# State product of a gated linear attention on four 64x64 places, value product in two parts

## The chip, the core and the metric

The kernel runs on one NeuronCore of a Trainium2 chip. The metric is the device time of one execution in microseconds (us). All engines of the core are in use: TensorE (PE in the profile) multiplies, VectorE (DVE), ScalarE (ACT) and GpSimd (POOL) do the rest, SyncE (SP) issues most transfers. TensorE writes its products to eight PSUM banks of 128 partitions x 512 floats.

## What is computed

The input is 4 sequences of 2048 tokens with 256 features. A layer norm is followed by a linear attention with 16 heads of 64 and a decaying state, a gate, an output projection and a residual; then comes a small network that is applied three times, with layer norms around both. The part that the change touches is the attention:

```python
Q = (xn @ WQ.T + bQ); K = (xn @ WK.T + bK); V = (xn @ WV.T + bV)     # 16 heads of 64
gate = silu(xn @ Wg.T + bg)
h = alpha * h + k[:, :, :, None] * v[:, :, None, :]    # token after token, h is 64x64 per head
o = einsum('bhi,bhij->bhj', q, h)
y = (o * gate) @ WO.T + bO
```

## The kernel before

Tokens are taken in **steps** of 512 (`NS` = 4 steps per sequence, 16 in all). A step projects its values first (`values`, 8 products of six matmuls), then goes through `NP` = 8 **pairs** of heads. A pair fills the 128 partitions: head e of the pair has the rows e*64 to e*64+63. Inside a pair the 512 tokens are `NC` = 4 **chunks** of 128, and the recurrence is replaced by matrix products for each chunk:

- `project` makes keys, queries and gate of the pair (six matmuls of 512 columns each, in split precision: high and low halves).
- `scores` multiplies keys and queries in 32-key blocks, each at 64x32 of the array; `masked` on DVE copies the causal part to `att`. In odd chunks the order of the 32-token blocks is reversed (the host prepares it so), so that the two chunks of a couple share one mask.
- `keys_transposed` turns the end-weighted keys `k_end` (made by POOL), ACT copies them to `k_tok` (`tokens_of`), `updates` multiplies them with the values, and DVE carries the state from chunk to chunk (`h_seq`, L758 and L762).
- `from_state` (L929) multiplies the state with the queries. The states of both heads stand in a block-diagonal 128x128 matrix `h_bd`, whose other two quarters are zero: four fp32 products of 128 columns.
- `from_chunk` (L938) adds the values times `att`: for each chunk and head one product of 128 keys, 64 outputs and 128 queries, two heads side by side in the array.
- `gated` on DVE multiplies bank 5 with the gate to `o_g` (L740), ACT and POOL split it into `o_hi` and `o_lo`, and `y_part` (L951, twelve matmuls of 256 columns) adds the pair's share of the output projection to banks 6 and 7.

An fp32 product is issued as two passes, so the trace has two MATMUL and two weight-load rows for each.

The order is written by hand, engine by engine, with semaphores; nothing is scheduled by a tool. TensorE's sequence of a pair p is: keys, queries and gate of pair p+1, `y_part(p-1)`, `from_state(p)`, `keys_transposed` of p+1, `from_chunk(p)`, `updates(p+1)`, `scores(p+1)`. Pair 6 has no `y_part`; pair 7 has two and a third follows the queries and gate of the next step's first pair. `x_transposed` (eight 128x128 transposes of the next step's normed input, in pair 6) and `x1_transposed` (eight of the last step's result, in pair 0) stand between. Banks: 0 and 1 keys, queries and gate in turn, 2 and 3 scores, 4 transposed keys and updates, 5 the output, 6 and 7 the output projection. After four steps comes the small network of that sequence, and `final_transposed` turns its result back.

Of the kernel before, what the change touches and what calls it, by code (L numbers as in the profile page):

```python
# [7 lines left out]
i32 = mybir.dt.int32  # L8
# [24 lines left out]
def build(nc, a, out):  # L33
    ctx = ExitStack()
    with ctx:
# [64 lines left out]
        h_bd = sb("h_bd", [P, NC, P])  # L100
# [41 lines left out]
        def k_bank(p):  # L142

            return p % 2

        def q_bank(p):

            return 1 - p % 2

        def g_bank(n):  # L150

            return n % NP % 2 if n else 5
# [44 lines left out]
        s_hbd = sem("state_diagonal_ready")  # L197
# [45 lines left out]
        started = [s_x1, s_out, s_og, s_xlo, s_upd, s_hbd, s_o, s_x1t, s_qev, s_kev, s_hs, s_x1c, s_ktok, s_att,  # L243
# [80 lines left out]
        def final_rows(t, c):  # L324

            return bank[(2, 0, 4, 6)[t] + c // 2][:, (c % 2) * D:(c % 2 + 1) * D]

        def v_bank(m):

            return bank[(2, 3, 5, 1, 2, 3, 0, 5)[m]]  # L330
# [7 lines left out]
        def _(pool):  # L338
# [47 lines left out]
            for b in range(B):  # L386
                for s in range(NS):
                    it = b * NS + s
                    following = it + 1 < B * NS
                    pool.wait_ge(s_x, (it + 1) * 16)  # L390
                    pool.wait_ge(s_x1, it + C0)
                    nc.gpsimd.tensor_tensor(x_2b[:], x_in[:], bias_o[:].unsqueeze(1).broadcast_to([P, NC, D]),
                                            ALU.add).then_inc(s_x2b, 1)
                    pool.wait_ge(s_x2b, it * 2 + 1)
                    nc.gpsimd.tensor_tensor(x_2b[:], x_2b[:], x_in[:], ALU.add).then_inc(s_x2b, 1)
                    pool.wait_ge(s_x2b, it * 2 + 2)
                    pool.sem_inc(s_xfree, 1)
                    for p in range(NP):
                        n = it * NP + p
                        if p + 1 < NP:  # L400
                            ends_of(p + 1, n + 1)
                        elif following:
                            ends_of(0, n + 1)
                        o_low(p, n)
                        if p == NP - 5 and following:
                            pool.wait_ge(s_stats, it + 2)
                            nc.gpsimd.tensor_tensor(rstd[:], vare[:], half_neg[:], ALU.pow).then_inc(s_rstd, 1)
                    pool.wait_ge(s_r1, it + 1)
# [12 lines left out]
        def _(act):  # L421
# [9 lines left out]
            def x_parts(step, banks_of):  # L431

                for k in range(KT):
                    act.wait_ge(s_xt, step * KT + k + 1)
                    if k == 0:
                        act.wait_ge(s_xlo, step + C0)
                    nc.scalar.activation(x_f[:, k, :], bank[banks_of[k]][:], ACT.Identity,
                                         bias=beta[:, k:k + 1], scale=gamma[:, k:k + 1]).then_inc(s_xf, 1)
                act.wait_ge(s_xf, (step + 1) * KT)
                nc.scalar.activation(x_hi[:], x_f, ACT.Copy).then_inc(s_xhi, 1)  # L440
# [18 lines left out]
            def tokens_of(n, bk):  # L459

                act.wait_ge(s_kt, n + 1 + C0)
                act.wait_ge(s_upd, n + C0)
                nc.scalar.activation(k_tok[:], part(bk, NC), ACT.Copy).then_inc(s_ktok, 1)  # L463

            def states_of(p, n):
# [3 lines left out]
                for e in range(2):  # L469
                    rows = slice(e * DH, (e + 1) * DH)  # L470
                    nc.scalar.activation(h_bd[rows, :, e * DH:(e + 1) * DH], h_seq[rows, :, :],  # L471
                                         ACT.Copy, scale=pows[rows, p, HP:HP + 1]).then_inc(s_hbd, 1)
# [7 lines left out]
            def x1_copied(step, first_bank):  # L480

                place = step % NS
                for k in range(KT):
                    act.wait_ge(s_x1t, step * KT + k + 1 + C0)
                    nc.scalar.activation(x1t[:, k, place * ST:(place + 1) * ST], bank[first_bank + k],
                                         ACT.Copy).then_inc(s_x1c, 1)
# [19 lines left out]
            x_parts(0, (0, 1))  # L506
# [8 lines left out]
            for b in range(B):  # L515
                for s in range(NS):
                    it = b * NS + s
                    following = it + 1 < B * NS
                    tokens_of(it * NP, 4)
                    for p in range(NP):  # L520
                        n = it * NP + p
                        states_of(p, n)
                        if p + 1 < NP:
# [3 lines left out]
                            tokens_of(n + 1, 4)  # L527
                            if p == 0 and s:
                                x1_copied(it - 1, 6)
                            if p == NP - 2 and following:  # L530
                                x_parts(it + 1, (0, 1))
                            o_high(p, n)
                        else:
                            o_high(p, n)
                            if following:
                                queries_shifted(0, n + 1)
                                act.wait_ge(s_og, n + C0)
                                gate_of(0, n + 1)

# [37 lines left out]
                for t in range(NS):  # L577
                    act.wait_ge(s_sh, b * NS + t + 1)
                    for c in range(NC):
                        last = nc.scalar.activation(fin[t][:, c, :], final_rows(t, c), ACT.Identity,  # L580
# [5 lines left out]
        def _(dve):  # L586
            nc.vector.memset(att[:].bitcast(i32), 0).then_inc(s_setv, 1)
            nc.vector.memset(h_bd[:].bitcast(i32), 0).then_inc(s_setv, 1)
            nc.vector.memset(bank[2], 0.0).then_inc(s_setv, 1)
            nc.vector.memset(bank[3], 0.0).then_inc(s_setv, 1)  # L590
# [3 lines left out]
            dve.wait_ge(s_setv, 7)  # L594
# [10 lines left out]
            def norm_stats(src, count, done, mv=mv[:], vare=vare[:]):  # L605

                for c in range(NC):
                    nc.vector.bn_stats(stats[:, c, :], src(c)).then_inc(s_st, 1)  # L608
                dve.wait_ge(s_st, count + NC)
# [589 lines left out]
```

## Time and profile before

| | us |
|---|---|
| median of 3 runs | 1869.63 (1869.55 to 1871.22) |
| the profiled execution | 1871.02 |
| its span, first to last instruction | 1869.3 |
| PE busy | 1792.7 (96% of the span) |
| DVE, ACT, POOL busy | 1076.9, 784.8, 483.1 |

A row of the timeline gives the start and the length of a run of like instructions. Matmuls overlap in the pipeline, so a run's length says little of what it costs; what counts is from the start of one run to the start of the next on the same engine. That is how TensorE's times are read below. The granted clock is at 2.4 GHz in all but the first and the last slice.

### The profile page before, as it was taken

To read this page: it belongs to the slowest core of one execution; us is meant where nothing else is said; L and a number is where in the kernel's file an instruction comes from. 1 tells how busy PE (TensorE), PEld (TensorE's weight loads), DVE (VectorE), ACT (ScalarE), POOL (GpSimd) and SP (SyncE) were. 2 spreads that over 40 slices of the span, in tenths; PEclk is the share of its full clock that TensorE was granted. 3 is DMA by queue.
4 is the path that set the end of the run, shared out by engine and by line. 5 is a ranking of instruction groups with operands and counts; after the bars stand their busy time and mean duration, and the time that the engine had idled before them with its cause. 6 is when DMAs were issued, how large, how long until landed. Compare 5 with 4: busy or idle time off the path is not lost.

```text
span 1869.3 us, 45361 instructions
## 1 busy us (share of the span) xinstructions
PE 1792.7 (96%) x19632; PEld 1383.2 (74%) x19632; DVE 1076.9 (58%) x2214; ACT 784.8 (42%) x1411; POOL 483.1 (26%) x373
## 2 busy tenths in 40 slices
PE   5999999999799999999979999999989999999996
PEld 4888888863588888885368888888438888888742
DVE  7565655555756555555665655555475555555546
ACT  3434343444443434344444343434444434343444
POOL 4232222212223222220222322222022222222202
PEclk9999999999999999999999999999999999999998
DMA  4000000000100000000010000000001000000001
GB/s 151 13 13 2 13 2 13 2 1 0 57 2 13 2 13 2 13 2 1 0 57 2 13 2 13 2 12 2 1 3 55 2 13 2 13 2 2 2 0 46
DMA packets 22823, 26.20 MB, mean 14 GB/s; under 512 B 3168, under 2 KB 21472, under 8 KB 22624
## 3 DMA queue, kind: packets, MB, share of 16 engines
q1 hardware_dynamic: 20624, 19.09, 3.2%
q10 hardware_dynamic: 2000, 4.20, 0.6%
q8 instruction: 156, 2.56, 0.6%
q14 instruction: 43, 0.35, 0.1%
HBM read 14.90 MB, written 8.39 MB: 12 GB/s over the span
## 4 chain that ended last, share of the span: by engine, by line
PE 92%; DVE 4%; ACT 2%; issue 1%; POOL 1%; DMA 0%; DVEq 0%; ACTq 0%; SPq 0%
PE bank L875 39%; PE bank L951 10%; PE bank L1110 9%; PE bank L938 7%; PE bank L902 6%; PE bank L929 6%; PE bank L1127 4%; PE bank L919 3%; PE bank L911 3%; PE bank L1153 1%; PE bank L1140 1%; DVE stats L608 1%; PE bank L866 1%; DVE v_sb L843 1%; PE bank L962 1%
## 5 line engine op out<-in xcount | busy, mean ns | idle before, releaser
L740 DVE TENSOR_TENSOR o_g<-bank,gate 128x512 f32<-128x512 f32 x128 | 88.6, 692 | 441.1 <-PE bank L938 441.1
L379 POOL TENSOR_TENSOR o_lo<-o_g,o_hi 128x512 fp32r<-128x512 f32 x128 | 166.0, 1297 | 659.7 <-ACT o_hi L478 659.7
L453 ACT ACTIVATE q_sb<-q_sb,pows 128x384 f32<-128x384 f32 (+2 forms) x384 | 168.2, 501 | 256.0 <-DVE q_sb L650 256.0
L370 POOL TENSOR_TENSOR k_end<-k_sc,pows 128x512 f32<-128x512 f32 x128 | 135.1, 1056 | 295.4 <-DVE k_sc L641 295.4
L471 ACT ACTIVATE h_bd<-h_seq,pows 64x256 f32<-64x256 f32 x256 | 130.6, 510 | 148.7 <-DVE h_seq L762 145.5
L463 ACT ACTIVATE k_tok<-bank 128x512 f32<-128x512 f32 x128 | 76.6, 598 | 243.6 <-PE bank L911 242.8
L729 DVE COPY_PREDICATED att<-causal,bank 128x1024 f32<-128x1024 int32 x128 | 168.6, 1317 | 6.2 <-PE bank L902 5.4
L478 ACT ACTIVATE o_hi<-o_g 128x512 fp32r<-128x512 f32 x128 | 80.7, 630 | 199.7 <-DVE o_g L740 199.5
L951 PE MATMUL bank<-wo_hi,o_hi 128*128 128x256 f32 x512 | 149.6, 292 | 2.8 <-POOL o_lo L379 2.8
L951 PE MATMUL bank<-wo_hi,o_lo 128*128 128x256 f32 x512 | 145.1, 283 | 0.0
L951 PE MATMUL bank<-wo_lo,o_hi 128*128 128x256 f32 x512 | 144.8, 283 | 0.0
L938 PE MATMUL bank<-att,v_sb 128*64 128x128 f32 x2048 | 140.1, 279 | 0.0
L929 PE MATMUL bank<-q_sb,h_bd 128*128 128x128 f32 x1024 | 137.4, 277 | 0.1
L929 PEld LDWEIGHTS bank<-q_sb,h_bd 128*128 128x128 f32 x1024 | 128.3, 192 | 5.9 <-ACT h_bd L471 3.0
L902 PE MATMUL bank<-q_sb,k_sc 64*32 64x64 f32 (+3 forms) x8192 | 128.1, 236 | 0.0
L938 PEld LDWEIGHTS bank<-att,v_sb 128*64 128x64 f32 x2048 | 109.2, 136 | 24.2 <-issue 24.1
L650 DVE SCALAR_TENSOR_TENSOR q_sb<-bank,col_bias,pows 128x512 f32<-128x512 f32 x128 | 96.1, 751 | 53.7 <-PE bank L875 53.6
L762 DVE SCALAR_TENSOR_TENSOR h_seq<-h_seq,pows,bank 128x64 f32<-128x64 f32 x384 | 107.9, 281 | 24.4 <-PE bank L919 2.0
L1110 PE MATMUL bank<-v_sb,f_w 128*128 128x512 f32 x256 | 121.0, 605 | 0.0
L875 PE MATMUL bank<-x_hi,wk_hi 128*128 128x512 f32 x256 | 113.2, 442 | 0.0
L902 PEld LDWEIGHTS bank<-q_sb,k_sc 64*32 64x32 f32 x8192 | 102.1, 106 | 14.2 <-issue 5.8
L722 DVE TENSOR_TENSOR v_sb<-bank,bias_v 128x512 f32<-128x512 f32 x128 | 85.0, 688 | 46.4 <-PE bank L875 45.7
(145 smaller groups left out, 3830.2 us busy)
## 6 DMA issues: line engine op xcount, KB each, us to landing
x_in<-in_x SPq DMA_DIRECT2D x16, 512.0 KB, 3.9
out_y<-q_sb SPq DMA_DIRECT2D x8, 512.0 KB, 2.8
out_y<-x_nf SPq DMA_DIRECT2D x8, 512.0 KB, 2.9
v_sb<-in_wq ACTq DMA_DIRECT2D x1, 1024.0 KB, 5.0
v_sb<-in_wk SPq DMA_DIRECT2D x1, 1024.0 KB, 8.8
x1t<-in_wg ACTq DMA_DIRECT2D x1, 1024.0 KB, 10.2
x1t<-in_wv ACTq DMA_DIRECT2D x1, 1024.0 KB, 13.1
q_sb<-in_wo ACTq DMA_DIRECT2D x1, 1024.0 KB, 17.1
```

Source lines behind the costliest of these rows:

```text
L370: nc.gpsimd.tensor_tensor(k_end[:].rearrange("p (a z) (b r) -> p a (z b) r", z=2, r=BL), k_sc[:].rearrange("p (a z) (b r) -> p a (z b) r", ...
L379: nc.gpsimd.tensor_tensor(o_lo[:, p % 2], o_g[:, p % 2], o_hi[:, p % 2].bitcast(f32), ALU.subtract).then_inc(s_olo, 1)
L453: last = nc.scalar.activation(q_sb[:, p % 2, d].rearrange("p (a z) n -> p a (z n)", z=2)[:, :, reach], q_sb[:, p % 2, 0].rearrange("p (a z ...
L471: nc.scalar.activation(h_bd[rows, :, e * DH:(e + 1) * DH], h_seq[rows, :, :], ACT.Copy, scale=pows[rows, p, HP:HP + 1]).then_inc(s_hbd, 1)
L729: nc.vector.copy_predicated(att[:].rearrange("p e (a z) n -> p (e a) (z n)", z=2), causal[:].bitcast(i32).rearrange("p z n -> p (z n)").un ...
L762: step = nc.vector.scalar_tensor_tensor(h_seq[:, c + 1, :] if c + 1 < NC else h_st[:, p, :], h_seq[:, c, :], pows[:, p, HP + 1:HP + 2], ba ...
L875: last = nc.tensor.matmul(dst, l(k), r(k), start=(m == 0), stop=(m == 5))
L902: last = nc.tensor.matmul(bank[2 + e][g * BL:(g + 1) * BL, cols:cols + count * BL], k_sc[rows, c, g * BL:(g + 1) * BL], query_blocks(rows, ...
L929: nc.tensor.matmul(bank[5][:, c * C:(c + 1) * C], h_bd[:, c, :], query_blocks(slice(0, P), p, c, first, NB), start=(c == 0), stop=False, s ...
L938: last = nc.tensor.matmul(bank[5][e * DH:(e + 1) * DH, c * C:(c + 1) * C], v_sb[:, c, h * DH:(h + 1) * DH], att[:, e, c, :], start=False, ...
L951: last = nc.tensor.matmul(dst, l[:, p % 2, tok], w[:, p, :], start=(p == 0 and c % 2 == 0 and i == 0), stop=(p == NP - 1 and i == 2), skip ...
L1110: last = nc.tensor.matmul(l1_bank(j, m)[:], f_w1[:, k, m * P:(m + 1) * P], src[:, k, tile_cols(t)], start=(k == 0), stop=(k == KT - 1))
```

## The change

The state product no longer uses the block-diagonal matrix. `h_sc` holds the scaled states of both heads below each other, and each chunk and head has a product of its own, 64 rows by 64 columns of the array. The column half is `(e + c) % 2`, so that two chunks with two heads take all four quarters. Even chunks' outputs go to bank 4, odd chunks' to bank 5. The value product is split: the 64 queries that come later in a chunk meet all 128 keys (128x64 of the array), the 64 that come first meet 64 keys (64x64). The first part is issued before `updates`, the second after it.

Around it nearly everything moves. Keys and gate share bank 0; queries, transposed keys and updates share bank 1; the values use banks 2 to 5. Transposes of the input, of the attention's result and of the final result go by row halves (`by_halves`): sixteen of 64 rows in place of eight of 128, the halves in two banks. `y_part` lags by one pair more, `x_transposed` moves from pair 6 to pair 5, `x1_transposed` from pair 0 to pair 1. On DVE `gated` becomes three instructions and stands behind the next pair's state steps; on ACT the copy of the input (`x_scaled`, `x_high`) is spread over pairs 5 and 6 and stands ahead of the token copy.

```diff
             def from_state(p):
                 for c in range(NC):
                     first = (NB - 1) * NC * C + c * C if c % 2 else c * C
-                    nc.tensor.matmul(bank[5][:, c * C:(c + 1) * C], h_bd[:, c, :],
-                                     query_blocks(slice(0, P), p, c, first, NB),
-                                     start=(c == 0), stop=False, skip_group_check=True)
+                    place = slice(c // 2 * C, (c // 2 + 1) * C)
+                    for e in range(2):
+                        rows = slice(e * DH, (e + 1) * DH)
+                        last = nc.tensor.matmul(bank[4 + c % 2][head_half(c, e), place], h_sc[rows, c, :],
+                                                query_blocks(rows, p, c, first, NB),
+                                                start=(c < 2), stop=False, skip_group_check=True)
...
+            def from_chunk(p, near):
                 for c in range(NC):
+                    early = slice(c % 2 * DH, c % 2 * DH + DH)
+                    late = slice(DH - c % 2 * DH, C - c % 2 * DH)
+                    keys, queries = (early, early) if near else (slice(0, P), late)
+                    first = c // 2 * C + queries.start
                     for e in range(2):
                         h = 2 * p + e
                         last = nc.tensor.matmul(
-                            bank[5][e * DH:(e + 1) * DH, c * C:(c + 1) * C],
-                            v_sb[:, c, h * DH:(h + 1) * DH], att[:, e, c, :],
+                            bank[4 + c % 2][head_half(c, e), first:first + DH],
+                            v_sb[keys, c, h * DH:(h + 1) * DH], att[keys, e, c, queries],
                             start=False, stop=True, skip_group_check=True)
...
+            def by_halves(first_bank, place, src):
+                for e in range(2):
+                    rows = slice(e * DH, (e + 1) * DH)
+                    last = nc.tensor.transpose(bank[first_bank + e][:, place * DH:(place + 1) * DH],
+                                               src[rows, :], ident[rows, rows])
+                return last
...
-                nc.vector.tensor_tensor(o_g[:, p % 2], bank[5], gate[:, p % 2, :], ALU.mult).then_inc(s_og, 1)
+                even = [by_places(tile[:, p % 2])[:, 0] for tile in (o_g, gate)]
+                nc.vector.tensor_tensor(even[0], part(4, NC)[:, 0:2], even[1], ALU.mult)
+                for e in range(2):
+                    rows = slice(e * DH, (e + 1) * DH)
+                    odd = [by_places(tile[rows, p % 2])[:, 1] for tile in (o_g, gate)]
+                    last = nc.vector.tensor_tensor(odd[0], part(5, NC)[head_half(1, e), 0:2], odd[1], ALU.mult)
+                last.then_inc(s_og, 1)
```

On TensorE, in pair 2 of a step: the end of `y_part`, then the small products up to the first of the scores. Before:

```order
L951 MATMUL bank<-wo_hi,o_lo 128x256
L929 MATMUL bank<-q_sb,h_bd 128x128 x4
L911 MATMUL bank<-ident,k_end 128x128 x4
L938 MATMUL bank<-att,v_sb 64x128 x8
L919 MATMUL bank<-v_sb,k_tok 64x64 x8
L902 MATMUL bank<-q_sb,k_sc 32x128 x2
```

and after:

```order
L998 MATMUL bank<-wo_hi,o_lo 128x256
L950 MATMUL bank<-ident,k_end 128x128 x4
L971 MATMUL bank<-q_sb,h_sc 64x128 x8
L985 MATMUL bank<-att,v_sb 64x64 x8
L958 MATMUL bank<-v_sb,k_tok 64x64 x8
L985 MATMUL bank<-att,v_sb 64x64 x8
L941 MATMUL bank<-q_sb,k_sc 32x128 x2
```

The key transposes stand ahead of the state product; the value product's first part (L985) keeps its place and its second part comes behind the updates.

On ScalarE, in pair 6 of a step, where the next step's input is copied: the shifted queries (`q_sb`), the gate, the token copy (`k_tok`), the input (`x_nf`, `x_hi`), the high half of the output (`o_hi`), the state (`h_bd`, `h_sc`). Before:

```order
L453 ACTIVATE q_sb<-q_sb,pows 128x2x64
L445 ACTIVATE gate<-bank,col_bias 128x512
L463 ACTIVATE k_tok<-bank 128x512
L437 ACTIVATE x_nf<-bank,beta,gamma 128x512 x2
L440 ACTIVATE x_hi<-x_nf 128x1024
L478 ACTIVATE o_hi<-o_g 128x512
L471 ACTIVATE h_bd<-h_seq,pows 64x4x64 x2
```

and after, from the gate of pair 5 to the token copy of pair 6:

```order
L460 ACTIVATE gate<-bank,col_bias 128x512
L449 ACTIVATE x_nf<-bank,beta,gamma 128x512 x2
L478 ACTIVATE k_tok<-bank 128x512
L484 ACTIVATE h_sc<-h_seq,pows 128x256
L490 ACTIVATE o_hi<-o_g 128x512
L468 ACTIVATE q_sb<-q_sb,pows 128x2x192
L468 ACTIVATE q_sb<-q_sb,pows 128x2x128
L468 ACTIVATE q_sb<-q_sb,pows 128x2x64
L460 ACTIVATE gate<-bank,col_bias 128x512
L455 ACTIVATE x_hi<-x_nf 128x1024
L478 ACTIVATE k_tok<-bank 128x512
```

The input's copies stood behind the token copy and now stand ahead of it, in two pairs.

On VectorE, a middle pair. Before, from the mask to the next pair's state steps:

```order
L729 COPY_PREDICATED att<-causal,bank 128x1024
L641 SCALAR_TENSOR_TENSOR k_sc<-bank,col_bias,pows 128x512
L650 SCALAR_TENSOR_TENSOR q_sb<-bank,col_bias,pows 128x512
L740 TENSOR_TENSOR o_g<-bank,gate 128x512
L758 COPY h_seq<-h_st 128x64
L762 SCALAR_TENSOR_TENSOR h_seq<-h_seq,pows,bank 128x64 x3
```

and after:

```order
L785 SCALAR_TENSOR_TENSOR h_st<-h_seq,pows,bank 128x64
L760 TENSOR_TENSOR o_g<-bank,gate 128x2x128
L764 TENSOR_TENSOR o_g<-bank,gate 64x2x128 x2
L660 SCALAR_TENSOR_TENSOR k_sc<-bank,col_bias,pows 128x512
L748 COPY_PREDICATED att<-causal,bank 128x1024
L669 SCALAR_TENSOR_TENSOR q_sb<-bank,col_bias,pows 128x512
```

The gating went behind the state steps, and the mask between keys and queries.

## Rows read from the trace of the kernel before

**Rows 1.** The page: busy time, share of the span and instructions of each engine.

```profile
PE 1792.7 (96%) x19632; PEld 1383.2 (74%) x19632; DVE 1076.9 (58%) x2214; ACT 784.8 (42%) x1411; POOL 483.1 (26%) x373
```

**Rows 2.** The page: shares of the chain that ended last, by engine.

```profile
PE 92%; DVE 4%; ACT 2%; issue 1%; POOL 1%; DMA 0%; DVEq 0%; ACTq 0%; SPq 0%
```

**Rows 3.** Stretches: length, busy PE, PEld, DVE, ACT, POOL, then PE's clock.

```profile
971.38:980.95 9.57, 9.57 (x143) 8.39 (x138) 4.25 (x9) 4.05 (x8) 1.47 (x2) 1.00 0.01 2
1018.29:1027.63 9.34, 9.19 (x139) 7.77 (x135) 4.53 (x10) 5.92 (x11) 2.36 (x2) 1.00 0.01 2
1027.06:1052.23 25.17, 25.17 (x279) 20.74 (x275) 17.04 (x34) 5.92 (x11) 9.45 (x6) 1.00 0.02 5
1052.23:1142.87 90.64, 90.52 (x1171) 77.20 (x1169) 51.33 (x109) 36.50 (x69) 25.63 (x20) 1.00 0.03 8
```

**Rows 4.** Timeline of PE, a middle pair: start, length, line and tile.

```profile
1086.91 1.05 PE L929 MATMUL bank<-q_sb,h_bd 128*128 128x128 f32 x8
1087.80 0.60 PE L911 MATMUL bank<-ident,k_end 128*128 128x128 f32 x4
1088.33 1.09 PE L938 MATMUL bank<-att,v_sb 128*64 128x128 f32 x16
1089.25 0.64 PE L919 MATMUL bank<-v_sb,k_tok 128*64 128x64 f32 x16
1089.82 1.00 PE L902 MATMUL bank<-q_sb,k_sc 64*32 64x128 f32 x64
1090.75 0.50 PE L875 MATMUL bank<-x_hi,wk_hi 128*128 128x512 f32 x1
```

**Rows 5.** Timeline of PE, pair 0 of another step and its projections.

```profile
1058.68 1.04 PE L962 MATMUL bank<-ident,x_nf 128*128 128x128 f32 x8
1059.65 1.09 PE L938 MATMUL bank<-att,v_sb 128*64 128x128 f32 x16
...
1062.07 0.51 PE L875 MATMUL bank<-x_hi,wk_hi 128*128 128x512 f32 x1
1062.41 0.39 PE L875 MATMUL bank<-x_lo,wk_hi 128*128 128x512 f32 x1
...
1066.36 0.28 PE L951 MATMUL bank<-wo_hi,o_hi 128*128 128x256 f32 x1
```

**Rows 6.** Timeline of DVE, a middle pair.

```profile
1079.91 0.69 DVE L740 TENSOR_TENSOR o_g<-bank,gate 128x512 f32<-128x512 f32 x1 [4.43 <-PE bank L938]
1080.52 0.18 DVE L758 COPY h_seq<-h_st 128x64 f32<-128x64 f32 x1
1080.81 0.91 DVE L762 SCALAR_TENSOR_TENSOR h_seq<-h_seq,pows,bank 128x64 f32<-128x64 f32 x3
...
1081.96 1.32 DVE L729 COPY_PREDICATED att<-causal,bank 128x1024 f32<-128x1024 int32 x1
1083.17 0.73 DVE L641 SCALAR_TENSOR_TENSOR k_sc<-bank,col_bias,pows 128x512 f32<-128x512 f32 x1
```

**Rows 7.** Timeline of ACT, pair 6 of a step.

```profile
1023.11 1.31 ACT L453 ACTIVATE q_sb<-q_sb,pows 128x384 f32<-128x384 f32 x3 [2.28 <-DVE q_sb L650]
1024.33 0.67 ACT L445 ACTIVATE gate<-bank,col_bias 128x512 f32<-128x512 f32 x1
1025.03 0.60 ACT L463 ACTIVATE k_tok<-bank 128x512 f32<-128x512 f32 x1
1025.81 1.45 ACT L437 ACTIVATE x_nf<-bank,beta,gamma 128x512 f32<-128x512 f32 x2 [0.18 <-PE bank L866]
1027.29 1.06 ACT L440 ACTIVATE x_hi<-x_nf 128x1024 fp32r<-128x1024 f32 x1
```

**Rows 8.** Chain of work, pair 0 of a sequence's first step: start, length.

```profile
962.08 2.99 PE bank L875 x12
...
967.31 0.76 ACT L445
...
969.84 0.69 PE bank L919 x16
```

More of the change, by code:

```diff
@@ L140, in query_blocks, with head_half, by_places, halves_of @@
             return bass.AP(view.tensor, view.offset + first, [list(view.ap[0]), [step, count], [1, BL]])
[L142 to L148, printed above, removed]
         def g_bank(n):
-            return n % NP % 2 if n else 5
+            return 0 if n else 5
+        def head_half(c, e):
+            first = (e + c) % 2 * DH
+            return slice(first, first + DH)
+        def by_places(rows):
+            return rows.rearrange("p (a z n) -> p z a n", z=2, n=C)
+        def halves_of(first_bank, first, count):
+            return psum[:, first_bank:first_bank + 2, first * DH:(first + count) * DH].rearrange(
+                "p r (c n) -> p c r n", n=DH)
+        def in_halves(rows):
+            return rows.rearrange("p (c r n) -> p c r n", r=2, n=DH)
         def part(n, k):
@@ L429, in weight_high, with x_scaled, x_high @@
                 nc.scalar.activation(w_hi[w][:], w_in[n], ACT.Copy).then_inc(s_whi, 1)
-            def x_parts(step, banks_of):
+            def x_scaled(step):
+                act.wait_ge(s_xt, step + 1)
+                act.wait_ge(s_xlo, step + C0)
                 for k in range(KT):
[L434 to L437, printed above, removed]
+                    nc.scalar.activation(in_halves(x_f[:, k, :]), halves_of(2, k * NC, NC), ACT.Identity,
                                          bias=beta[:, k:k + 1], scale=gamma[:, k:k + 1]).then_inc(s_xf, 1)
+            def x_high(step):
                 act.wait_ge(s_xf, (step + 1) * KT)
@@ L468, in states_of @@
                 act.wait_ge(s_o, n + C0)
[L469 to L472, printed above, removed]
+                nc.scalar.activation(h_sc[:], h_seq[:], ACT.Copy, scale=pows[:, p, HP:HP + 1]).then_inc(s_hsc, 1)
             def o_high(p, n):
@@ L505, in _ @@
             act.wait_ge(s_first, 16 * len(first_consts))
-            x_parts(0, (0, 1))
+            x_scaled(0)
+            x_high(0)
             for n, w in enumerate("kgv"):
@@ L906, in scores, with keys_transposed @@
                 return last
-            def keys_transposed(bk):
+            def keys_transposed():
                 for c in range(NC):
-                    last = nc.tensor.transpose(bank[bk][:, c * C:(c + 1) * C], k_end[:, c, :], ident[:])
+                    last = nc.tensor.transpose(bank[1][:, c * C:(c + 1) * C], k_end[:, c, :], ident[:])
                 return last
@@ new lines, in _ @@
+                            if p == 1 and s:
+                                x1_transposed(it - 1, 6)
+                        else:
+                            y_part(p - 2, n - 2)
+                            if following:
+                                pe.wait_ge(s_gev, n + 1)
+                                pe.wait_ge(s_xlo, it + 2 + C0)
+                                project("k", 0, 0).then_inc(s_k, 1)
+                        pe.wait_ge(s_hsc, n + 1 + C0)
+                        pe.wait_ge(s_og, n + C0)
```

246 lines of the change are left out of this document (127 added, 119 removed).

## The prediction

> **What bounds the kernel now.** I read the page first. PE is busy for 96% of the span [rows 1], and 92% of the chain that ended last is PE's [rows 2]. Then the stretches, all at the full clock of 2.4 GHz (1.00): a middle pair takes 9.57 us and PE is busy in all of it; a whole step takes 90.64 us, 90.52 of them busy [rows 3]. In that step DVE works 51.33 us, ACT 36.50. So TensorE sets the time, and what a product costs is the distance from its start to the start of the next run.
>
> In a middle pair [rows 4] these distances are: state product 1087.80 - 1086.91 = 0.89, key transposes 0.53, value product 0.92, updates 0.57, scores 0.93, together 3.84 us. The three projections take 1066.36 - 1062.07 = 4.29 [rows 5], and the output part the rest, 9.57 - 4.29 - 3.84 = 1.44.
>
> From these I take the unit costs. Eight 128-column passes in 0.89 are 0.11 each. The four transposes would be 0.44 at that rate and take 0.53: **0.09 for leaving the 128*128 form** for 128*64. The value product is 16 passes, two side by side, so 8 places of 0.11, and 0.04 more for the first weights, which nothing hides behind a switch. The updates leave for 64*32, so 0.57 - 0.09 = 0.48 for 8 places of 64 columns: 0.06 each. The first 512-column matmul behind a switch takes 0.34, the second 0.23 [rows 5]: first weights of 128 columns cost 0.11.
>
> **The pair's products.** State product: 16 passes on four quarters are 4 places of 128 columns, 4 x 0.11 + 0.04 first weights + 0.09 to leave = 0.57 in place of 0.89. Value product, later queries: 16 passes, two side by side, 64 columns, 8 x 0.06 + 0.04 = 0.52; no switch to the updates, which have the same form (0.57 with their leaving). First queries: 16 passes on four quarters, 4 x 0.06 + 0.04 + 0.09 = 0.37. So the value product goes from 0.92 to 0.89: the quarter of the columns that it saves pays for two switches. Transposes 0.53 and scores 0.93 stay. Sum 3.49 for 3.84: **0.35 saved per pair**, 9.22 for 9.57. Four quarters at once appear nowhere in the trace. The nearest row for it is the scores': eight places of 64*32 run there at once. Each place has 2 x 320 columns, 5 x 0.11 = 0.55 by the unit costs; 0.93 less 0.09 and 0.04 is 0.80, 1.45 times that. So I bound the two four-place products between full overlap (0.44 and 0.24) and 1.45 times it (0.64 and 0.35), and take the first, since two side by side in rows 4 run at full rate; the upper end costs 0.31 more per pair.
>
> **Transposes by halves.** Eight took 1059.65 - 1058.68 = 0.97 [rows 5]. Now the form changes on entry (0.09, first weights 0.11) and on leaving (0.09). Sixteen of 64 rows, two at a time, are 8 places; their moving side has 64 columns (0.06), but their weights still have 128 columns, and the load of those takes 0.11. I take 0.11: 0.88 + 0.29 = 1.17, and 0.11 for the first weights of whatever 128*128 product follows, 1.28. That is +0.3 us a block. Bounds: 0.06 a place (-0.1), and halves that load one after the other (+1.2).
> The Trainium skill ("TensorE: Matmul & The Clock Gate", LDWEIGHTS) states that a weight load costs by its columns and not by its rows, 107 ns for 128 at its formula; the 0.11 of rows 5 agrees. By a price per row the block would gain 0.1.
>
> **Who else must be in time.** I walk through a pair with 0 at the start of its key projection. DVE: the state steps end near 0.05 (updates start at -1.87, take 0.57 and some 0.2 until DVE sees them, and four steps take 1.15 [rows 6]). Gating in three instructions of 256 elements: the one of 512 costs 0.61 to the next start, so some 0.4 each, bounds 0.3 and 0.6; 1.2. Keys are projected at 1.54; DVE takes them at 1.73, for 0.7; then the mask, 1.21 from start to start [rows 6]; queries 3.61 to 4.36. ACT: shifted queries 1.22, gate 0.70 [rows 7], so 6.3; token copy 0.60, 6.95, and the updates can start at **7.0**. TensorE gets there at 4.29 + 1.44 + 0.53 + 0.57 + 0.52 = 7.35. In pairs 2 to 4 nothing waits, with 0.35 to spare. But:
> - Pair 0 has no output part and no `x1_transposed` any more: TensorE is there at 6.1 and waits till 7.0. Updates to updates: 0.6 + 7.0 = 7.6. Before, 90.64 - 5 x 9.57 - 9.34 - 25.17 = 8.3.
> - Pair 1 has the transposes in place of the output part: 7.15, so 7.15 + 1.87 (updates, first queries, scores) = 9.0.
> - Pair 5: 9.22 + 1.28 = 10.5. The input copy (1.45) delays the token copy to 8.45, and the updates are due at 8.6: hidden.
> - Pair 6: `x_high` (1.06, some 0.1 of it beside its neighbour) stands ahead of the token copy: updates at 7.95, not 7.35. 7.95 + 1.87 = 9.8; before 9.34 without an output part.
> - Pair 7 and the values: 25.17 before. It gains the 0.35 and loses it to switches (queries and scores no longer follow the same forms): 25.2.
>
> A step: 7.6 + 9.0 + 3 x 9.22 + 10.5 + 9.8 + 25.2 = **89.8 against 90.64**, 0.85 saved; twelve steps are of this kind: -10. In a sequence's first step ACT loads a table in pair 0 (0.76 of it on the chain [rows 8], more than that in all) ahead of the gate; before, the updates came 969.84 - 962.08 = 7.8 after the key projection's start, now the queries are 0.45 later, 8.3: 8.9; pair 1 8.9 without transposes; together 91.0 against 90.8: +1 for four. Four blocks of x1 and four of final transposes outside the pairs at +0.3: +2. POOL keeps its work, 25.63 us a step [rows 3]; its residual sums now sit in pair 1 behind `k_end`, ahead of nothing that pair 2 needs early. DMA is idle. The shorter setup is too small to count. Sum -7: the profiled execution's 1871.0 becomes 1864, and on the median 1869.6 - 7 = **1863**. The order takes back what the four places give: 0.35 x 8 = 2.8 us of products per step, less 0.6 for transposes, less 0.9 and 0.6 for waits that were hidden.
>
> **Rivals.**
> - **Cheaper transposes** (0.2): 0.06 a place. Saves 0.4 in pair 5 (15 times), 0.15 in pair 1 (12 times, then the token copy binds), 0.4 in eight blocks outside: -11, 1852. For it: the moving side is halved; against: the load's 0.11.
> - **Token copy late in more pairs** (0.12): the three gatings cost 0.6 each, queries 0.4 later, pair 6 and pair 1 later by 0.4 and 0.2: +9, 1872, no change. For it: reads from other partitions, in three pieces; against: rows 6 has DVE idle 4.43 us a pair.
> - **Four places don't fully overlap** (0.14): 0.31 more in six pairs of eight, some 0.1 in the two that wait: 2.0 a step, +32, **1895, slower than before**. It decides from 0.09 us a pair on. For it: scores run at 1.45 times their columns; against: the two-place runs don't.
> - **Halves of rows follow each other in the transposes** (0.1): +0.9 in some 35 blocks, +31, 1894, slower.
> - **The bank rule** (0.08): the tiles (rows 0, columns 0) and (rows 64, columns 64) of the state product write the same bank at once, in different partitions. If that serializes, it takes 0.88 + 0.13, +0.44 per pair, in six pairs of eight: +42, 1905. Against it: in the value product of rows 4 both column halves write bank 5 at once at full rate; but they have the same rows of the array. The Trainium skill ("TensorEngine Tiling (Array Packing)", Restrictions and Gotchas, Gotcha 1) states that different row tiles cannot access the same PSUM bank at the same time, which would be this case; no row of before shows such tiles on one bank.
>
> **How the numbers follow.** Main case 0.36, 1863, own range 1856 to 1870. A change under 0.2%, 3.7 us, can't be told from none in this kernel: main gives 0.24 faster and 0.12 same. Faster: 0.24 + 0.2 = 0.44; same: 0.12 + 0.12 = 0.24; slower: 0.14 + 0.1 + 0.08 = 0.32. The range takes in the cheap transposes with some switch time less (1845) and the two rivals near 1895, and leaves out the bank rule: 1845 to 1896.
>
> **What would show it.** In the changed profile: state product start to start 0.57 (0.9 or more: bank rule; 0.77: partial overlap), value parts 0.52 and 0.37; a middle pair 9.22; transposes block 1.28 (0.9 cheap, over 2 serial); updates waiting for the token copy about 0.9 us in pair 0, 0.6 in pair 6 and none in pairs 2 to 4. The prediction is wrong if updates wait in middle pairs, if DVE or ACT take over the chain, or if a switch costs other than 0.09.

## The result, and the profile after

| | before | after |
|---|---|---|
| median | 1869.59 (4 runs) | **1841.93** (1838.94 to 1842.75, 4 runs) |
| span of the profiled execution | 1869.3 | 1837.2 |

The ratio is 0.9847, with a 95% interval of 0.983 to 0.9864: 1.5% faster. I had forecast 1863, with a range from 1845; the time lies below the range. The direction was right and the size four times too small: 28 us where I had 7. The profiled execution of after is its fastest; its other three runs are 3 to 4 us longer, so differences of medians below and differences of spans don't agree to better than that.

The page of after, with the rows that answer to [rows 1] and [rows 2]:

```profile
PE 1743.2 (95%) x23088; PEld 1302.1 (71%) x23088; DVE 1123.4 (61%) x2467; ACT 709.1 (39%) x1283; POOL 478.4 (26%) x373
PE 83%; DVE 7%; ACT 6%; issue 3%; DMA 0%; POOL 0%; ACTq 0%; DVEq 0%; SPq 0%
```

TensorE works 50 us less, and of the chain 16% now lies on DVE, ACT and issue, where it was 7%. The span is 32 us shorter: the gain is made on TensorE, and some of it is lost to waits. The stretches that answer to [rows 3], from the start of one pair's updates to the next: a middle pair (4), pairs 0, 1, 5, 6 and 7, a whole regular step, then the program's very first step. The columns are those of rows 3.

```profile
1156.28:1165.55 9.27, 9.27 (x169) 7.87 (x166) 6.38 (x15) 3.62 (x7) 2.40 (x3) 1.00 0.01 2
1121.63:1128.99 7.36, 6.90 (x74) 5.16 (x70) 5.13 (x12) 2.87 (x6) 1.06 (x1) 1.00 0.01 2
1128.99:1137.70 8.71, 8.71 (x166) 6.97 (x168) 5.02 (x11) 3.56 (x8) 4.72 (x4) 1.00 0.01 2
1165.55:1175.61 10.06, 10.06 (x184) 8.32 (x182) 5.01 (x11) 4.84 (x9) 2.32 (x2) 1.00 0.01 2
1175.61:1185.21 9.60, 9.41 (x169) 7.87 (x165) 5.42 (x11) 4.45 (x8) 2.31 (x2) 1.00 0.02 3
1185.21:1210.18 24.97, 24.97 (x315) 20.68 (x315) 16.03 (x35) 4.26 (x8) 4.64 (x4) 1.00 0.01 1
1033.15:1121.63 88.48, 87.85 (x1379) 72.56 (x1377) 54.88 (x125) 31.75 (x61) 25.31 (x20) 1.00 0.03 8
44.28:132.83 88.55, 87.44 (x1365) 72.07 (x1361) 53.60 (x121) 30.79 (x59) 25.31 (x20) 1.00 0.03 8
```

The clock is at 1.00 in all of them, so all differences are of work or of waits. Against the prediction (us, start of updates to start of updates):

| | before | predicted | after |
|---|---|---|---|
| pair 0 | 8.34 | 7.6 | 7.36 |
| pair 1 | 9.57 | 9.0 | 8.71 |
| pairs 2 to 4, each | 9.57 | 9.22 | 9.24 to 9.32 |
| pair 5 | 9.57 | 10.5 | 10.08 |
| pair 6 | 9.33 | 9.8 | 9.60 |
| pair 7 and values | 25.14 | 25.2 | 24.97 |
| regular step | 90.65 | 89.8 | 88.5 |
| first step of sequences 1 to 3 | 90.8 | 91.0 | 89.95 |
| the very first step | 93.34 | 0.2 longer | 88.55 |
| the rest between two sequences | 94.2 | +0.6 | 94.65 |

Twelve regular steps at -2.15, three first steps at -0.85, the very first at -4.8 and three gaps at +0.45 are -31.8, of the 32.1 by which the spans differ. Pairs 3 and 4 were hit within 0.05 us, pair 2 within 0.1; everything round them went better than I had said.

Single pairs are longer than their like in several of the kernels. Where the excess is 1.3 to 1.4 us (pair 1 in a sequence's first step, once or twice in the traces of e_full_transposes, e_pool_first, e_state_128, e_swap and e_best), the granted clock over the pair is 0.82 or 0.83: for 3.4 us of it TensorE has 1.2 GHz and not 2.4. In e_full_transposes, whose pair 1 otherwise takes 8.71 there:

```profile
1405.25:1415.36 10.11, 8.68 (x130) 6.87 (x134) 5.93 (x11) 3.48 (x8) 4.08 (x3) 0.83 0.00 1
```

Why the clock falls in one execution and not in the next isn't shown. Other single pairs are 0.2 to 0.7 us longer at a clock of 1.00; their cause stays open.

TensorE's timeline in a middle pair of after, which answers to [rows 4], and then the input's transposes in pair 5, which answer to [rows 5]:

```profile
1163.90 0.60 PE L950 MATMUL bank<-ident,k_end 128*128 128x128 f32 x4
1164.44 0.67 PE L971 MATMUL bank<-q_sb,h_sc 64*64 64x128 f32 x16
1165.03 0.69 PE L985 MATMUL bank<-att,v_sb 128*64 128x64 f32 x16
1165.55 0.64 PE L958 MATMUL bank<-v_sb,k_tok 128*64 128x64 f32 x16
1166.12 0.46 PE L985 MATMUL bank<-att,v_sb 64*64 64x64 f32 x16
1166.51 1.00 PE L941 MATMUL bank<-q_sb,k_sc 64*32 64x128 f32 x64
1167.44 0.50 PE L914 MATMUL bank<-x_hi,wk_hi 128*128 128x512 f32 x1
...
1171.81 0.71 PE L898 MATMUL bank<-ident,x_nf 64*128 64x64 f32 x16
1172.45 0.38 PE L998 MATMUL bank<-wo_hi,o_hi 128*128 128x256 f32 x1
1172.67 0.28 PE L998 MATMUL bank<-wo_lo,o_hi 128*128 128x256 f32 x1
```

From start to start: state product 0.59 (predicted 0.57), the value product's parts 0.52 and 0.39 (0.52 and 0.37), updates 0.57, scores 0.93. **Four quarters do run at once**, at the full rate. The transposes take 0.64, and here is the first large miss.

### The profile page after: what moved, and what is told of

The parts are those of the page before. It is cut to its first block, busy times and chain, and to the rows that moved or that the text cites. A ratio compares the mean times of both kernels' runs of the same rounds, so it can differ in the third digit from the quotient of the medians.

```text
span 1837.2 us, 52404 instructions
## 1 busy us (share of the span) xinstructions
PE 1743.2 (95%) x23088; PEld 1302.1 (71%) x23088; DVE 1123.4 (61%) x2467; ACT 709.1 (39%) x1283; POOL 478.4 (26%) x373
## 3 DMA queue, kind: packets, MB, share of 16 engines
HBM read 14.90 MB, written 8.39 MB: 13 GB/s over the span
## 4 chain that ended last, share of the span: by engine, by line
PE 83%; DVE 7%; ACT 6%; issue 3%; DMA 0%; POOL 0%; ACTq 0%; DVEq 0%; SPq 0%
PE bank L914 34%; PE bank L1159 9%; PE bank L998 9%; PE bank L941 6%; PE bank L985 6%; PE bank L1176 5%; PE bank L958 4%; PE bank L971 3%; PE bank L950 2%; DVE att L748 2%; ACT q_sb L468 2%; PE bank L1202 1%; DVE q_sb L669 1%; PE bank L1189 1%; PE bank L898 1%
## 5 line engine op out<-in xcount | busy, mean ns | idle before, releaser
L484 ACT ACTIVATE h_sc<-h_seq,pows 128x256 f32<-128x256 f32 x128 | 65.2, 509 | 407.6 <-DVE h_seq L785 407.6
L985 PE MATMUL bank<-att,v_sb 128*64 128x64 f32 (+1 forms) x4096 | 145.7, 229 | 0.3 <-DVE att L748 0.3
L985 PEld LDWEIGHTS bank<-att,v_sb 128*64 128x64 f32 (+1 forms) x4096 | 111.5, 135 | 31.1 <-issue 21.8
L660 DVE SCALAR_TENSOR_TENSOR k_sc<-bank,col_bias,pows 128x512 f32<-128x512 f32 x128 | 96.1, 750 | 56.9 <-PE bank L914 56.9
L941 PE MATMUL bank<-q_sb,k_sc 64*32 64x32 f32 (+3 forms) x8192 | 128.8, 236 | 0.6 <-issue 0.6
L764 DVE TENSOR_TENSOR o_g<-bank,gate 64x256 f32<-64x256 f32 x256 | 107.9, 421 | 3.4
L914 PE MATMUL bank<-wv_hi,x_hi 128*128 128x512 f32 x256 | 105.0, 410 | 3.4 <-POOL wv_lo L378 2.0
L914 PE MATMUL bank<-x_hi,wq_hi 128*128 128x512 f32 x256 | 103.1, 403 | 4.1 <-DVE x_lo L655 4.1
L914 PE MATMUL bank<-wv_lo,x_hi 128*128 128x512 f32 x256 | 103.7, 405 | 0.0
```

The lines of the kernel that those rows point to most:

```text
L660: nc.vector.scalar_tensor_tensor(k_sc[:].rearrange("p c (b r) -> p (c b) r", r=BL), bank[0].rearrange("p (c r) -> p c r", r=BL), col_bias[ ...
L764: last = nc.vector.tensor_tensor(odd[0], part(5, NC)[head_half(1, e), 0:2], odd[1], ALU.mult)
L914: last = nc.tensor.matmul(dst, l(k), r(k), start=(m == 0), stop=(m == 5))
L941: last = nc.tensor.matmul(bank[2 + e][g * BL:(g + 1) * BL, cols:cols + count * BL], k_sc[rows, c, g * BL:(g + 1) * BL], query_blocks(rows, ...
L985: last = nc.tensor.matmul(bank[4 + c % 2][head_half(c, e), first:first + DH], v_sb[keys, c, h * DH:(h + 1) * DH], att[keys, e, c, queries] ...
```

## The experiments

### The transposes

Whole ones in after, and halves alone in before.

```diff
 # e_full_transposes: after, with
...
+                k, c = place // NC, place % NC
+                return nc.tensor.transpose(bank[first_bank + k][:, c * P:(c + 1) * P], src, ident[:])
...
```

> The changed kernel with one part undone: input, attention result and final result are transposed again by eight 128x128 products a block in place of sixteen 64-row ones. New theory: a block by halves costs 0.64 us from start to start plus 0.08 for each switch beside it; undone it costs 0.86 plus 0.1 for leaving, so pair 1 gets 0.2 us and pair 5 some 0.1 us longer, in all +4 to +6 us over the changed kernel, ratio to before about 0.988. The prediction's term (1.28 us a block by halves, against 0.97): undoing it would make the kernel 8 to 10 us faster, ratio about 0.980.

Measured: 1845.5 us, 0.9868 (0.9853 to 0.9882) of before, so 3.6 us more than after by the medians; the intervals of the two ratios overlap. In e_full_transposes, pair 5, then pair 1:

```profile
1169.49:1179.59 10.10, 10.10 (x176) 8.66 (x174) 5.01 (x11) 4.84 (x9) 2.32 (x2) 1.00 0.01 2
1132.81:1141.74 8.93, 8.93 (x159) 7.22 (x160) 5.01 (x11) 3.80 (x8) 4.94 (x4) 1.00 0.01 2
```

Pair 5 is the same with either (10.10 and 10.08), pair 1 gains 0.22 by halves, where a switch of form stands in any case. I had halves 0.4 dearer than 0.88; they take 0.64 with the switch on leaving, 0.09 for the switch on entry and 0.10 for the first weights of the output part (1172.67 - 1172.45 = 0.22, then 0.12 a matmul), 0.83 in all (10.08 - 9.25), and eight whole ones 0.85. So the term was wrong by 0.4 in pair 5. Added up over the pairs, without the one at the lower clock, the halves bring 3 to 4 us, most of it in pair 1 of regular steps.

```diff
 # b_halves: before, with
...
+                        last = by_halves(0, k * NC + c, x_n[:, c, k * P:(k + 1) * P])
+                last.then_inc(s_xt, 1)
...
```

> The kernel before with one part of the change alone: the three kinds of transposes by row halves. New theory: a block costs 0.64 and 0.09 for leaving the 128*128 form ahead of it, in place of 0.97; two blocks a step, 0.25 each: 6 to 9 us faster than before, ratio about 0.996. The prediction's term (+0.3 us a block): 10 us slower, ratio 1.005.

Measured: 1872.87 us, 1.0016 (1.0007 to 1.0025). Neither theory had this: no gain, though pair 6 goes from 9.33 to 8.97 and pair 0 from 8.34 to 8.11. Pair 7 takes it all back, 25.79 for 25.14. Where it goes shows in POOL's and DVE's timelines at that place, in before and then in b_halves:

```profile
1028.95 1.29 POOL L379 TENSOR_TENSOR o_lo<-o_g,o_hi 128x512 fp32r<-128x512 f32 x1 [5.88 <-ACT o_hi L478]
...
1029.32 2.00 DVE L636 TENSOR_TENSOR x_lo<-x_nf,x_hi 128x1024 fp32r<-128x1024 f32 x1
```

```profile
1028.94 1.22 DVE L647 TENSOR_TENSOR x_lo<-x_nf,x_hi 128x1024 fp32r<-128x1024 f32 x1
...
1028.99 2.30 POOL L389 TENSOR_TENSOR o_lo<-o_g,o_hi 128x512 fp32r<-128x512 f32 x1 [5.95 <-ACT o_hi L488]
```

Whichever comes first runs at its own speed (1.29 or 1.22), and the other one lasts longer by most of what is left of it: DVE's by 0.78 of 0.92 us, POOL's by 1.01 of 1.17. In before POOL was 0.37 us ahead, and DVE's longer time was hidden. In b_halves DVE is 0.05 us ahead, and the output's low half comes 1 us later; the chain of b_halves goes through it:

```profile
1028.30 0.63 ACT o_hi L488
1028.93 0.07 issue
1028.99 2.31 POOL o_lo L389
1031.30 0.04 issue
1031.35 1.71 PE bank L969 x12
```

One step of b_halves has it the other way round: there POOL is 0.03 us ahead, and pair 7 takes 25.24 in place of the 25.76 to 25.80 of the others.

```profile
1668.03 1.28 POOL L389 TENSOR_TENSOR o_lo<-o_g,o_hi 128x512 fp32r<-128x512 f32 x1 [5.95 <-ACT o_hi L488]
1668.06 2.33 DVE L647 TENSOR_TENSOR x_lo<-x_nf,x_hi 128x1024 fp32r<-128x1024 f32 x1
```

To test the collision, b_halves_mask puts one other DVE instruction ahead of `x_lo`:

```diff
 # b_halves_mask: b_halves, with DVE's mask of pair 7 ahead of the input's low half
+                            masked(n)
                             ...
-                            masked(n)
```

> The kernel before with transposes by halves, and in pair 7 DVE's mask ahead of its low part of the next input, nothing else. Theory: the transposes gave their 0.25 to 0.35 us a block, but in pair 7 DVE's x_lo then started 0.05 us ahead of POOL's o_lo and held it up (2.30 us in place of 1.29), and the output part waited for it; with the mask between them o_lo takes 1.3 us again, pairs 6 and 7 together 34.1 us in place of 34.8, and the whole is 7 to 10 us faster than before, ratio 0.9945 to 0.9965. Rival (the collision is incidental, halves cost what they save): ratio 1.0016 as without it.

Measured: 1864.34 us, 0.9971 (0.9959 to 0.9983). Pair 7 falls to 25.2, `o_lo` takes 1.29 or 1.30 again in every step, and the program is 8.5 us faster than b_halves. The collision is the cause. Halves and this order together are worth 5 us in before; this order without halves was not run. The mask itself, beside POOL's `o_lo`, takes 1.33, no longer than elsewhere. The Trainium skill ("SBUF — State Buffer", Who interferes with whom) says that a DVE instruction with two SBUF inputs contends with a GpSimd instruction that reads SBUF, and that issue order decides which of the two blocks; these rows agree.

### The very first step

In before its pair 0 takes 11.04 us (8.44 in other sequences), in after 7.36. Two things lengthen it. The first is a collision. POOL's and DVE's rows there, first of before, then DVE's of b_pool_later, then POOL's and DVE's of e_pool_first:

```profile
45.21 2.40 POOL L395 TENSOR_TENSOR x_2b<-x_2b,x_in 128x1024 f32<-128x1024 f32 x1
...
45.50 2.17 DVE L758 COPY h_seq<-h_st 128x64 f32<-128x64 f32 x1
```

```profile
45.44 0.18 DVE L768 COPY h_seq<-h_st 128x64 f32<-128x64 f32 x1
```

```profile
42.64 2.39 POOL L407 TENSOR_TENSOR x_2b<-x_in,bias_o 128x1024 f32<-128x1024 f32 x1
...
43.79 1.30 DVE L790 COPY h_seq<-h_st 128x64 f32<-128x64 f32 x1
```

A copy of 64 columns (0.18 us in [rows 6]) lasts until POOL's sum ends: 45.50 + 2.17 = 47.67 against 45.21 + 2.40 = 47.61; with it the state steps, the keys and the queries come 2 us later. Here the same page and section of the Trainium skill says that copies can take the pair of ports shared with GpSimd; 2.17 for 0.18 agrees.

The second is the clock. Pair 0 of the very first step, in before and then in b_halves, whose copy is as long (2.12):

```profile
44.10:55.14 11.04, 9.09 (x65) 7.49 (x64) 5.82 (x8) 3.61 (x7) 4.50 (x3) 0.85 0.15 47
44.05:53.47 9.42, 7.51 (x66) 6.13 (x64) 5.79 (x8) 3.49 (x7) 4.46 (x3) 1.00 0.17 57
```

In before the granted clock is at half, 1.2 GHz, for 3.4 us from 50.2 on, after TensorE had stood idle for 2 us; a 512-column matmul takes 0.43 there and not 0.23. In b_halves TensorE stands idle as long and the clock stays. So of the 3.6 us above b_pool_later's 7.46 the copy makes 2.0 and the clock 1.6.

```diff
 # b_pool_later: before, the residual sums of step 0 in pair 1, behind k_end (there where after has them)
...
+                    if it:
                         nc.gpsimd.tensor_tensor(x_2b[:], x_in[:], ...)
...
+                        if it == 0 and p == 1:
+                            nc.gpsimd.tensor_tensor(x_2b[:], x_in[:], ...)
```

> The kernel before, with POOL's two residual sums of the very first step moved from the step's start behind the end-weighted keys of pair 2; nothing else moved. Theory: in the first step DVE's 0.18 us copy of the state takes 2.17 us beside POOL's second sum, and the keys' end weights wait behind the sums, and pair 0 takes 11.04 us where the others take 8.4; so 2.5 to 3.7 us faster, ratio 0.998 to 0.9987. Rival (start-up of another kind): no change.

Measured: 1867.11 us, 0.9982 (0.9973 to 0.999), as expected in size, though by the traces 1.6 us of it are the clock's; pair 0 takes 7.46 at a clock of 1.00. The reverse in after:

```diff
 # e_pool_first: after, the residual sums of step 0 back in pair 0
+                        if p == 0 and it == 0:
+                            nc.gpsimd.tensor_tensor(x_2b[:], x_in[:], ...)
```

> The changed kernel, with POOL's residual sums of the very first step moved back to the step's start. Theory: pair 0 of that step takes 3 to 4 us longer, updates to updates 7.36 to about 10.9, +3 to +4 us over the changed kernel, ratio about 0.9865. Rival: no change, 0.985.

Measured: 1841.21 us, 0.9846 (0.9833 to 0.9858): no change, a miss. The copy is blocked again, 1.30 us, but after does this copy before the mask and not behind it, in a time in which DVE would wait 0.77 us for the updates, and pair 0 takes 7.46. So moving POOL's sums mends this place in before, and in after the place of the copy is enough without it.

### The state product

```diff
 # e_state_128: after, with four products of 128x128 and two ACT copies into a matrix with zero quarters
+                    last = nc.tensor.matmul(bank[4 + c % 2][:, place], h_bd[:, c, :],
+                                            query_blocks(slice(0, P), p, c, first, NB), ...)
```

> The changed kernel with the state product at 128x128 again, block-diagonal for even chunks and anti-diagonal for odd ones, two ACT instructions a pair in place of one. Theory: from start to start 0.98 us in place of 0.60 and the key transposes 0.44 in place of 0.53, so +0.29 us a pair; in pairs 0 and 6 the wait for the token copy takes it up; 6 x 16 x 0.29 = +28 us over the changed kernel, ratio about 0.9995. Rival (the four places give little and the new order is what gains): under +10 us, ratio 0.990 or less.

Measured: 1868.06 us, 0.9987 (0.9978 to 0.9996). Without the four quarters all the rest of the change is worth 2 us against before. A pair of e_state_128, and its rows (key transposes 0.43, state product 0.99):

```profile
1076.37:1085.91 9.54, 9.54 (x161) 8.36 (x159) 6.88 (x20) 4.12 (x8) 3.32 (x3) 1.00 0.01 3
```

```profile
1083.97 0.60 PE L958 MATMUL bank<-ident,k_end 128*128 128x128 f32 x4
1084.40 1.06 PE L977 MATMUL bank<-q_sb,h_bd 128*128 128x128 f32 x8
1085.39 0.69 PE L991 MATMUL bank<-att,v_sb 128*64 128x64 f32 x16
```

Product and transposes together are 1.42 where after has 1.13: 0.29 us in pairs 2 to 5, 0.24 in pair 7. In pairs 0 and 6 the wait for the token copy takes it up; in pair 1 of regular steps, where the product stands behind the transposes by halves, it is 0.49 (1.09 us for 0.60). That makes 26 us by the medians. This is the one part that carries the change.

### The split of the value product

```diff
 # e_whole: after, with the value product in one part, ahead of the updates
-                        from_chunk(p, False)
+                        from_chunk(p).then_inc(s_o, 1)
...
-                        from_chunk(p, True).then_inc(s_o, 1)
```

> The changed kernel with the value product whole again: per chunk and head 128 keys, 128 queries at 128x64, all issued ahead of the updates. Prediction's term: the split saves 0.03 us a pair, since the quarter of the columns pays for two switches and first weights; so +0 to +4 us over the changed kernel, ratio 0.985 to 0.987. Rival (the split is where the unforeseen 21 us came from): +20 us, ratio 0.996.

Measured: 1831.41 us, 0.9792 (0.9777 to 0.9806). Both theories missed: **the split costs 10 us** (7.6 in the spans of the two profiled executions). A middle pair is the same (9.27), as the unit costs say (0.92 whole, 0.52 + 0.39 in parts). But the second part stands behind the updates: it no longer fills the time in which TensorE waits for the token copy, and it puts off the next key projection, from which the next token copy's chain starts. Pair 6 goes from 9.60 to 9.25, pairs 7 and 0 together from 32.33 to 31.89, and pair 1 of a sequence's first step from 8.71 to 8.39. Pair 1 of regular steps gets longer, 8.71 to 9.03. In e_whole, its timeline there:

```profile
1041.01 0.40 PE L914 MATMUL bank<-x_hi,wg_lo 128*128 128x512 f32 x1
1041.67 0.65 PE L950 MATMUL bank<-ident,k_end 128*128 128x128 f32 x4 [0.27 <-POOL k_end L382]
```

The last matmul of the gate takes 0.23 in pairs where nothing is awaited, and 0.66 here: the key transposes wait for POOL's `k_end`. Its timeline:

```profile
1039.31 1.29 POOL L391 TENSOR_TENSOR o_lo<-o_g,o_hi 128x512 fp32r<-128x512 f32 x1 [7.09 <-ACT o_hi L490]
1040.57 1.05 POOL L382 TENSOR_TENSOR k_end<-k_sc,pows 128x512 f32<-128x512 f32 x1
```

`o_lo`, which nobody needs before pair 2, stands ahead of it.

### The order of DVE and POOL

```diff
 # e_swap: after, DVE's queries ahead of its mask in all pairs but 5
+MASK_FIRST = (NP - 3,)
...
-                            masked(n)
+                            if p in MASK_FIRST:
+                                masked(n)
...
                             queries_of(p + 1, n + 1)
+                            if p not in MASK_FIRST:
+                                masked(n)
```

> The changed kernel with one order changed on DVE: in all pairs but pair 5 the queries are taken before the mask, so they are ready some 0.42 us earlier. Theory: in pairs 0 and 6 the updates wait 0.64 and 0.35 us for the token copy, which hangs on these queries; both waits shrink by up to 0.42 and 0.35, in all 10 to 13 us faster than the changed kernel, ratio about 0.978. Rival (these waits have another cause, or the mask becomes late instead): no change, ratio 0.985.

Measured: 1828.17 us, 0.9774 (0.9757 to 0.979). The token copy's chain runs keys, mask, queries, shifted queries, gate, token copy; without the mask in it pair 0 takes 7.00 for 7.36 and pair 6 9.25 for 9.60. Its pair 0 and a regular step:

```profile
1026.27:1033.27 7.00, 6.71 (x74) 5.25 (x71) 5.08 (x12) 2.87 (x6) 1.05 (x1) 1.00 0.01 4
1026.27:1113.96 87.69, 87.40 (x1380) 72.54 (x1377) 57.00 (x125) 31.77 (x61) 25.29 (x20) 1.00 0.03 8
```

With the value product whole in pair 7 alone, and then whole everywhere:

> The changed kernel with queries before the mask (all pairs but 5) and, in pair 7 alone, the value product whole, since no updates stand beside it there and the split has two more switches. Theory: the gain of the order alone (to about 0.9775) and 0.45 us a step more, 16 times, -7 us: ratio 0.973 to 0.974, 1821 us. Rival (pair 7's gain in the kernel with the whole value product came from earlier pairs): ratio 0.9775.

Measured: 1827.19 us, 0.9771 (0.9758 to 0.9784): nothing gained over e_swap, where I had expected 7 us. Pair 7 takes 24.90 to 24.96 (24.94 in e_swap, 24.51 in e_whole): this stretch begins with the second part of pair 6's product, which e_best still has.

> The changed kernel with both: queries before the mask (all pairs but 5), and the value product whole ahead of the updates in every pair. Theory: the whole product is worth nothing by itself, it fills the wait for the token copy in pairs 0 and 6 with 0.4 us of work; once the order has shortened these waits, little is left: -1 to -4 us against the order alone, ratio 0.975 to 0.977. If the two gains were independent, -10 and -14 us would add up: ratio 0.972 or less.

Measured: 1825.67 us, 0.9754 (0.974 to 0.9767), 2.5 us less than e_swap. The gains of 14 and 10 us overlap in pair 6 (9.25 with either, 9.28 with both). In pair 7 the whole product adds 0.38 (24.94 to 24.56), but in regular steps pair 1 takes it back: 9.03, where e_swap has 8.62. So the last kernel moves POOL's work:

```diff
 # e_ends_first: e_swap_whole, with k_end ahead of o_lo on POOL in pair 1
+                        if p == 1:
+                            ends_of((p + 1) % NP, n + 1)
                         if p:
                             o_low(p - 1, n - 1)
-                        if p + 1 < NP or following:
+                        if p != 1 and (p + 1 < NP or following):
```

> e_swap_whole with one POOL order changed: in pair 1 of a step POOL makes the end-weighted keys (k_end) of pair 2 ahead of the low half of the output (o_lo). With the value product whole, the trace shows the key transposes of pair 1 waiting 0.27 us for k_end, which POOL starts only behind o_lo (1.29 us). Theory: this wait is the 0.3 us by which pair 1 of a regular step takes 9.03 instead of 8.71. Then pair 1 takes 8.7 in 12 steps of 16, the program 3 to 4 us less than e_swap_whole: ratio to before 0.973 to 0.974. Rival: the token copy binds right behind it, or the missing time is taken from somewhere else in the pair: pair 1 stays at 9.0 with the wait now at the updates, ratio 0.975 to 0.976.

Measured: **1816.49 us, 0.9716 (0.9703 to 0.9729)**, the fastest of all, and 7 to 9 us less than e_swap_whole (by the ratios and by the medians) where I expected 3 to 4. Pair 1 of e_ends_first, and a whole regular step:

```profile
1026.73:1035.27 8.54, 8.54 (x154) 7.07 (x152) 7.07 (x13) 4.24 (x9) 4.46 (x3) 1.00 0.01 2
1019.73:1107.01 87.28, 87.28 (x1251) 73.04 (x1249) 57.85 (x125) 31.81 (x61) 25.29 (x20) 1.00 0.03 8
```

I had read the 0.27 of the row as the whole wait. By starts it was 0.66 - 0.23 = 0.43, and pair 1 gains 0.5 in all 16 steps (9.03 to 8.54; in first steps 8.39 to 7.89): 8 us. The program is now as fast as if both gains had added up (1842 - 14 - 10 = 1818). In the profile of a whole regular step TensorE has no idle time left (87.28 of 87.28).

After has 0.39 at this place, and in pair 0 as well as in pair 1. That is another wait. In pair 0 `k_end` is ready 0.9 us ahead, and the key transposes (1126.69) start 0.14 us after DVE's copy of the queries (1125.81 + 0.74), for which they wait too, since both use bank 1. In e_swap, where this copy comes earlier, pair 0 has 0.23.

## Why the prediction was wrong

**Right.** What bounds: TensorE, start to start. The unit costs: state product, both value parts, the switch of 0.09, the middle pair (9.25 for 9.22). Gating in three pieces (0.43 each, by 0.42 and 0.85 in the rows below, in pair 1 of after). The waits in pairs 0 and 6 are there, though shorter (0.62 and 0.36 us start to start, where I had 0.9 and 0.6), and none in pairs 2 to 4.

```profile
1130.88 0.42 DVE L760 TENSOR_TENSOR o_g<-bank,gate 128x256 f32<-128x256 f32 x1
1131.31 0.85 DVE L764 TENSOR_TENSOR o_g<-bank,gate 64x256 f32<-64x256 f32 x2
```

Four rivals fell: partial overlap (0.59 and not 0.77), halves one after the other (0.64 and not over 2), late gating, and the bank rule. Even chunks' outputs of both row halves go to bank 4, in different partitions, at the full rate: 16 passes in 0.59. The Trainium skill ("TensorEngine Tiling (Array Packing)", Restrictions and Gotchas, Gotcha 1) says that different row tiles cannot access the same PSUM bank simultaneously; this trace shows them there in other partitions with no loss of time, so the measurement decides against that rival.

**Wrong, by its own steps.** The spans differ by 32.1 us and I had 7. The terms below make 24 us of the 25; pairs 2 to 4, 0.04 us longer than forecast, take off 2, and the rest is rounding, the gaps and single long pairs of before. The price of the four quarters was right; what failed are terms round it:

1. *Transposes by halves* (6 us in pair 5, and part of 4 us in pair 1, which came 0.2 to 0.3 shorter). I took 0.11 a place for the weight load; the trace has 0.64 for eight places, so about 0.06 each, and a load of 64 rows cost no more than that. The Trainium skill ("TensorE: Matmul & The Clock Gate", LDWEIGHTS) has the load by columns alone, which I had taken as agreeing with [rows 5]. Those rows have 128 rows and 128 columns in one; they could not tell the two prices apart. This trace disagrees with the page. It was my rival with 0.2; by itself it gave 1852, still 10 us too slow.
2. *The walk to the token copy* (6 us in pairs 0 and 6, and the other part of pair 1). I took ACT's gate at 0.70 from [rows 7], where its next instruction had come 0.70 later because it waited for TensorE. Where nothing waits, the next start is 0.57 later (1183.06 to 1183.63 in ACT's rows of pair 6 below). The queries came as walked. The rest is a few hundredths in the token copy and in what I rounded up; all in all pair 0's updates came 6.75 us behind the key projection's start (1122.24 to 1128.99) and not 7.0.
3. *The very first step* (4 us in its pair 0). I costed it like other first steps and never looked at its pair 0, though [rows 3] stood for regular steps only. Its 11.04 for 8.44 was in the trace, with the lengthened copy and the clock of 0.85. The 1.6 us of the clock are not owed to the change: b_halves, with the order of before in this place, is without them too.
4. *Pair 7* (3 us, 0.23 a time): 24.97 for 25.2. I let switches eat the 0.35; they ate half.

```profile
1181.85 1.31 ACT L468 ACTIVATE q_sb<-q_sb,pows 128x384 f32<-128x384 f32 x3 [2.45 <-DVE q_sb L669]
1183.06 0.67 ACT L460 ACTIVATE gate<-bank,col_bias 128x512 f32<-128x512 f32 x1
1183.63 1.04 ACT L455 ACTIVATE x_hi<-x_nf 128x1024 fp32r<-128x1024 f32 x1
1184.58 0.58 ACT L478 ACTIVATE k_tok<-bank 128x512 f32<-128x512 f32 x1
```

The misses all had one sign: where a cost was open I took the dearer end or the row with a wait in it. The walk to the token copy had no bounds of its own in the range, though 0.25 us there is worth 8 us. And where I wrote that the split pays for its switches, I asked only what the products cost, not what the second part keeps from starting: 10 us, which e_whole shows.

## What to carry to other kernels

A piece of matrix work is worth more ahead of a wait than behind it: before a product is split, ask which wait the moved part used to fill and which chain starts behind it. The idle time in brackets can be less than the wait: compare the start-to-start distance of the row before it with the same row in a pair that doesn't wait, and look at the queue order of every engine that the waiting one depends on. Before a longer stretch is put down to an order or a collision, read its granted clock. Unit costs of a product can be taken from start-to-start distances to a few hundredths of a microsecond, but only from rows that change one size at a time and wait for nothing.

## What the runs showed of the hardware

- Four 64x64 quarters run at once at full rate: 16 passes of 128 columns in 0.59 us, against 0.89 for 8 passes on the whole array.
- Transposes of 64 rows by 128 weight columns, two at a time: 16 passes in 0.64 us; eight passes of 128 rows took 0.85 between products of their own form and 0.97 ahead of another.
- Some DVE instructions and POOL's sums and differences in SBUF exclude each other nearly for whole instructions: a 0.18 us copy lasted 2.17, a 1.22 us difference of two SBUF tensors 2.00, POOL's 1.29 us difference 2.30. DVE's mask, which reads the scores' bank, wasn't lengthened beside it (1.33). A lead of 0.05 us decides which one pays, and it cost b_halves 8 us.
- A stretch of 3.4 us at a granted clock of 1.2 GHz made a pair 1.3 to 1.6 us longer, in some traces and not in others of the same order.
